# The first layer's direct term moved to its last three stages, product copies ahead of byte codes, and the second layer begun before the last turn

## What is computed

```python
# first layer, K = 4
terms = [x, L @ x]
for _ in range(2, K):
    terms.append(2.0 * (L @ terms[-1]) - terms[-2])
out = einsum('kni,kio->no', stack(terms), weight)
x = layernorm(x + out)
# second layer, as far as it matters here
(adj > 0) @ h, (adj < 0) @ h, adj+ @ h, adj- @ h     # then gates of two GRU cells
```

## The kernel before

| stage | visits | passes | beside the product |
|---|---|---|---|
| start, B | 0-31 | 0; in B also 1 | masks, counts, row sums |
| C | 32-41 | 1, quarter 2 (and two tiles of 3) | codes 0, row sums |
| D | 42-49 | 1, quarter 1 | counts 1, row sums |
| E | 50-57 | 1, and from 52 also 2, quarter 0 | counts 2, codes 1, row sums |
| F | 58-67 | 2, quarters 0 and 1 | codes 2 |
| G | 68-75 | 2, quarter 2 | counts 3, row sums |
| H | 76-83 | 2, quarter 3 | codes 3 |

## Time and profile before

### The profile page before, as it was taken

One profiled execution on the slowest core, in us unless ns is written; L12 is line 12 of the kernel. 1 busy time (PEld: TensorE's weight loads), 2 busy tenths in 40 slices (PEclk: granted clock), 3 DMA queues, 4 the chain that ended last, 5 costly groups with the idle time before them and its releaser, 6 DMA issues. The chain is left out here.

```text
span 1476.3 us, 18448 instructions
## 1 busy us (share of the span) xinstructions
PE 1330.1 (90%) x6874; PEld 592.6 (40%) x6874; DVE 1203.3 (82%) x1560; ACT 984.5 (67%) x919; POOL 222.7 (15%) x150
## 2 busy tenths in 40 slices
PE   5899998999899899999999999989987888888893
PEld 1233334333334354454544554544433433333342
DVE  5898989995865887877977977458688899899997
ACT  0001442894583678567577768677689899999985
POOL 1000000000000000000000001143133445444550
PEclk9999999999999999999999999999979999999995
DMA  9999979988999565544535533143633656556610
GB/s 361 409 409 410 370 264 377 411 346 318 413 410 412 212 234 193 189 147 177 193 134 187 193 138 105 61 148 134 215 114 115 213 158 227 178 166 215 217 54 29
DMA packets 134561, 341.56 MB, mean 231 GB/s; under 512 B 7877, under 2 KB 57481, under 8 KB 134281
## 3 DMA queue, kind: packets, MB, share of 16 engines
q1 hardware_dynamic: 118240, 320.88, 59.4%
q10 hardware_dynamic: 16232, 19.51, 3.9%
HBM read 321.49 MB, written 17.83 MB: 230 GB/s over the span
## 5 line engine op out<-in xcount | busy, mean ns | idle before, releaser
L1088 PE MATMUL ps<-ring,X 128*64 128x512 f32 x512 | 234.1, 605 | 15.4 <-DVE ring L2444 10.2
L1089 PE MATMUL ps<-work,X 128*64 128x512 f32 x512 | 234.2, 605 | 0.0
L844 POOL TENSOR_TENSOR ring<-ring,work 128x1024 f32<-128x1024 f32 x72 | 170.1, 2363 | 223.6 <-DVE work L2836 223.6
L1684 ACT ACTIVATE work<-ring 128x2048 f32<-128x2048 f32 x64 | 122.5, 1913 | 79.4 <-PE ps L1104 31.8
L821 POOL TENSOR_SCALAR work<-ring 128x1024 int16<-128x1024 uint8 x24 | 27.5, 1148 | 963.5 <-DMA ring<-codes 888.2
L951 PE MATMUL ps<-ring,work 128*64 128x512 f32 x704 | 162.6, 610 | 1.5 <-DVE Y L2102 1.5
L2444 DVE TENSOR_SCALAR ring<-ring 128x2048 f32<-128x2048 f32 x64 | 78.4, 1225 | 66.6 <-ACT work L1684 66.1
L1088 PEld LDWEIGHTS ps<-ring,X 128*64 128x64 f32 x512 | 67.1, 139 | 152.1 <-issue 141.8
L2124 DVE TENSOR_TENSOR work<-work,ring 128x1024 f32<-128x1024 f32 (+1 forms) x98 | 108.0, 1102 | 8.5 <-DMA ring<-in_adjT 6.6
L1493 ACT ACTIVATE work<-work,code_bias 128x2048 uint8<-128x2048 bf16 (+1 forms) x32 | 62.2, 1944 | 66.8 <-DVE work L2163 53.5
L1267 PE MATMUL ps<-work 64*128 64x512 f32 x288 | 88.6, 694 | 17.4 <-DVE work L2851 15.9
(11 more groups left out here) (387 smaller groups left out, 2708.1 us busy)
## 6 DMA issues: line engine op xcount, KB each, us to landing
ring<-in_adjT SPq DMA_DIRECT2D x86, 2048.0 KB, 11.3
work<-in_adjT SPq DMA_DIRECT2D x26, 2048.0 KB, 22.3
ring<-in_adjT SPq DMA_DIRECT2D x24, 1024.0 KB, 8.8
ring<-in_adjT SPq DMA_DIRECT2D x48, 512.0 KB, 3.8
ring<-codes SPq DMA_DIRECT2D x32, 512.0 KB, 3.8
ring<-in_adjT SPq DMA_DIRECT2D x64, 256.0 KB, 3.1
codes<-work ACTq DMA_DIRECT2D x32, 256.0 KB, 6.5
codes<-work ACTq DMA_DIRECT2D x64, 128.0 KB, 2.7
```

The source lines that it names most:

```text
L844: nc.gpsimd.tensor_tensor(u.edges[:, cols], u.edges[:, cols], u.angle[:, cols], ALU.mult).then_inc(weighted, 1)
L1088: nc.tensor.matmul(ps[0:F, h, :], rows, ring[:, r, 2 * (m % 2) + i, cols], start=start, stop=stop)
L1089: mm = nc.tensor.matmul(ps[F:P, h, :], rows, negs[:, m % 2, i, cols], start=start, stop=stop)
L1684: nc.scalar.activation(negs[:, pair], ring[:, r, 2 * pair:2 * pair + 2, :], ACT.Relu, scale=-1.0).then_inc(negs_made, 1)
```

## The change

- The direct term moves from visits 37-40 to 60-63 (`FIRST_AT`), with its reads one visit later. Its transfer is now two of 512 KB, one for each half of the partitions, issued by ACT at visit 57, behind the copy of turn 7; x's transposed form lies in T1's room, which has had its last reader then. It uses banks 0 and 1, and turn 11 uses banks 6 and 7.
- The signs of visit 42 wait for nothing of the direct term. `att_weights` goes to banks 2 and 3 and waits for the first counts' read instead of turn 3's. The first normalisation moves one visit later (62).
- On ACT, where the visit ahead of a turn has codes (turns 5 and 9), the copy of the product comes ahead of those codes.
- Turn 11 and its two copies move behind pair 0 of the second layer, on PE behind `mask_products` of pair 0. What pair 0 writes over waits for the room's last reader by name.
- The six rooms are dealt so that the last visits 78, 79, 80, 81, 82 and 83 use rooms 1, 5, 4, 3, 2 and 0. The order in which tiles are loaded is as before.

The diff, cut to its core:

```diff
-        xT_sb = signs_words[0:F, :]
+        xT_sb = work[:, 0:NB * F]
...
-        TURN_BANKS = (0, 4, 0, 4, 0, 6, 4, 0, 6, 4, 0, 4)
+        TURN_BANKS = (0, 4, 0, 4, 0, 6, 4, 0, 6, 4, 0, 6)
...
-        WEIGHTS_AT, ATT_AT, FIRST_AT = C_AT + 2, C_AT + 4, C_AT + 5
-        NORMS_AT = (F_AT + 3, G_AT + 1, H_AT + 1)
+        ATT_AT, FIRST_AT = C_AT + 4, F_AT + 2
+        NORMS_AT = (F_AT + 4, G_AT + 1, H_AT + 1)
...
+        place = {r: p for r, p in zip(sorted(range(RING0), key=lambda r: last_use[r]), (1, 5, 4, 3, 2, 0))}
+        for a in visits:
+            a.slot = place[a.slot]
...
             def first(n):
                 if n == 0:
-                    pe.wait_ge(xT_in, 16)
-                if n < 2:
-                    pe.wait_ge(first_read, 1)
-                else:
+                    pe.wait_ge(xT_in, 32)
+                    pe.wait_ge(turn_read, 8)
+                if n >= 2:
                     pe.wait_ge(first_read, 1 + 2 * (n - 1))
+                rows = slice(n // 2 * F, (n // 2 + 1) * F)
                 for c in range(8):
-                    b = n * 8 + c
-                    mm = nc.tensor.matmul(ps[:, 4 + n % 2, c * F:(c + 1) * F], xT_sb[:, b * P:(b + 1) * P], w_first[:],
+                    b = n % 2 * 8 + c
+                    mm = nc.tensor.matmul(ps[:, n % 2, c * F:(c + 1) * F], xT_sb[rows, b * P:(b + 1) * P], w_first[rows],
...
-            turn(LAST_TURN)
             pe.sem_inc(pair_used, 2)
...
+                    if q == 0 and m == 0:
+                        turn(LAST_TURN)
...
                 if m and a.sign_n == NS:
                     act.wait_ge(based, SLOTS)
-                    act.wait_ge(first_read, 9)
+                    act.wait_ge(first_read, 1)
...
-                if a.t in TURNS_AT:
+                if a.t in TURNS_AT and not visits[a.t - 1].chain:
                     copy_product(act, TURNS_AT.index(a.t))
...
-                if a.t == C_AT:
-                    act.wait_ge(based, SLOTS)
-                    act.wait_ge(counts_made, NS)
-                    act.dma_start(xT_sb, xT).then_inc(xT_in, 16)
...
                 if a.t == F_AT - 1:
                     copy_product(act, 7)
-                if a.t == len(visits) - 1:
-                    copy_product(act, LAST_TURN)
+                    for h in range(2):
+                        act.dma_start(xT_sb[h * F:(h + 1) * F, :], xT[:, h * (N // 2):(h + 1) * (N // 2)]).then_inc(xT_in, 16)
+                if a.chain and a.t + 1 in TURNS_AT:
+                    copy_product(act, TURNS_AT.index(a.t + 1))
                 if a.chain:
                     make_codes(a)
...
-                    act.wait_ge(pair_used, q * PAIRS + m + 1)
+                    if q == 0 and m == 0:
+                        act.wait_ge(tile_multiplied, visits[slot_after[4]].multiplied)
+                    else:
+                        act.wait_ge(pair_used, q * PAIRS + m + 1)
```

More of the change, by code:

```diff
@@ L598, in adjacency_stack @@
             last_use[a.slot] = t
-            a.room = ring[:, a.slot] if a.slot < RING else spare[:, a.slot - RING]
             a.turns = [NQ * p + (a.q if p != 1 else NQ - 1 - a.q) for p in a.passes]
@@ L617, in adjacency_stack @@
                 signed_n += 1
+        place = {r: p for r, p in zip(sorted(range(RING0), key=lambda r: last_use[r]), (1, 5, 4, 3, 2, 0))}
+        for a in visits:
+            a.slot = place[a.slot]
+            a.room = ring[:, a.slot] if a.slot < RING else spare[:, a.slot - RING]
+        slot_after = [max(a.t for a in visits if a.slot == r) for r in range(RING0)]
         turns0 = 3 * NQ
-        slot_after = last_use[0:RING]
         def quarter_blocks(q):
@@ L867, in att_weights @@
                 pe.wait_ge(weights_made, 2)
[L868 to L872 removed]
+                pe.wait_ge(counts_read, 1)
+                nc.tensor.matmul(ps[:, 2, 0:2], gatWT_sb[:], gat_a_sb[:], start=True, stop=True)
+                nc.tensor.matmul(ps[:, 2, F:2 * F + 1], w3_pick[:], w3_words[0:F, :], start=True, stop=True)
+                nc.tensor.matmul(ps[0:F, 2, 3 * F:4 * F + 1], move_pick[:], w3_words[0:F, :], start=True, stop=True)
+                nc.tensor.matmul(ps[:, 3, 0:3 * F], gatWT_sb[:], winT_sb[:], start=True, stop=True).then_inc(
                     gat_ready, 1)
@@ L897, in count @@
                         pe.wait_ge(counts_read, m)
+                        pe.wait_ge(first_read, 1)
                 for h in range(2):
@@ L937, in multiply @@
                     pe.wait_ge(base_read, 2 * NQ)
-                if a.begins[i] and n == 6:
+                if a.begins[i] and n == 10:
                     pe.wait_ge(first_read, 9)
@@ L1687, in _ @@
                         act.wait_ge(negs_made, q * PAIRS + m + 1)
+                        if q == 0 and m == 0:
+                            act.wait_ge(tile_multiplied, visits[slot_after[3]].multiplied)
                         nc.scalar.activation(less[:, pair], negs[:, pair], ACT.Sign).then_inc(less_made, 1)
+                    if q == 0 and m == 0:
+                        copy_product(act, LAST_TURN)
                     make_codes1(q, m)
@@ L2422, in _ @@
                         mine = own_blocks(ring[:, r], s % 2, pair)
+                        if m == 0 and q == 0:
+                            dve.wait_ge(tile_multiplied, visits[slot_after[5]].multiplied)
                         V.tensor_tensor(own, mine, ident[:].unsqueeze(1).broadcast_to([P, 2, P]),
@@ L2438, in _ @@
                     if m % 2:
+                        if q == 0 and m == 1:
+                            dve.wait_ge(tile_multiplied, visits[-1].multiplied)
                         if s // 2 == q:
@@ L2447, in _ @@
                         make_more(q, m, edges).then_inc(masks_made, 1)
+                    if q == 0 and m == 0:
+                        copy_product_dve(LAST_TURN)
                     if q == 0 and m == 2:
```

32 lines of the change are left out of this document (12 added, 20 removed).

## The result

The changed kernel takes 1481.75 us in the median of 20 runs (1475.91 to 1491.39), the kernel before 1477.53 us on the same chip: ratio 1.0029, 95% interval 1.0018 to 1.0041. A second comparison on another chip gave 1483.22 against 1478.16, ratio 1.0037 (1.0023 to 1.0051). It is about 0.3% slower; 1480.3 us was forecast, with a range of 1473.5 to 1485.

A forecast was written before the change was run, and what follows sets the result against it. PE was taken to bound stages D and E and the stretch from pair 0, transfers F to H. Terms -1.65 + 2.9 + 0 + 2.05 = +3.3 us on the median 1477.05 gave 1480.3 us, range 1473.5 to 1485.

The forecast's parts named there:

- Turn 5 and count 42: Stage C to D: count 42 1.65 us earlier, clock loss after PE's idles 2.9 us, so stage E ends 1.25 us later.
- the clock holds: Rival at turn 5: the idles there cost no clock; +0.4 us in all, 1477.5 us; chance 0.15.
- the codes' transfer isn't the gate: Faster rival: visit 42's signs don't wait for that transfer, count starts 4.5 us earlier; down to 1472.3 us; chance 0.17.
- The direct term in stage F: Visits 60 to 63: the added PE and DVE work stays hidden and the stream of tiles unbroken; cost 0.
- the slower rival: Stage F: clock falls behind three narrow pieces, stream of tiles breaks, 3.3 us lost, 1483.7 us; chance 0.23.
- The turn behind pair 0: Start of second layer: turn 11 now stands on PE where it has no gap, nothing gained; +2.05 us.
- Ahead of pair 0: Sign at the passage to the second layer: PE idle for 3 to 5 us before pair 0.

The follow-up runs named there:

- e7: Changed kernel plus useless matmuls on PE around turn 5, 7 ahead and 4 behind; 1479.55 us, ratio 1.0003 to the kernel before.
- after: First profile of the changed kernel, no further edit; the profiled execution spans 1478.4 us (1480.17 as a run).
- e12: Changed kernel run again with no edit, on another chip; 1483.22 us, ratio 1.0037 to the kernel before.
- e1: Changed kernel with turn 11 and its copies back ahead of pair 0; 1482.31 us, ratio 1.0037 to the kernel before.
- e5: Changed kernel with x's transfer cut to an eighth (128 KB in place of 1 MB); 1481.20 us, ratio 1.0025 to the kernel before.
- e9: Changed kernel with the direct term one visit later in stage F; 1483.80 us, ratio 1.0040 to the kernel before.
- e10: Changed kernel, signs of 42 and 68 before codes, turn 11 back, direct term one visit later, useless matmuls around turn 5 (7 and 1); 1470.91 us, ratio 0.9957.
- e6: Changed kernel with signs of visits 42 and 68 ahead of codes of 41 and 67, turn 11 back ahead of pair 0; 1475.27 us, ratio 0.9980.
- e8: Changed kernel, direct term back in stage C, signs of 42 and 68 before codes, turn 11 back ahead of pair 0; 1479.00 us, ratio 1.0009.
- e11: Changed kernel, signs of 42 and 68 before codes, turn 11 back ahead of pair 0, direct term one visit later in F; 1473.19 us, ratio 0.9969.

## Why the prediction was right, and where it wasn't

The total was right (+3.3 forecast, +4.2 in the medians with an interval of 2.7 to 6.1), but that is luck: two terms were set too high and one at nothing, and the errors cancelled. The three below come to +3.4 us; no column tells where the other 0.8 of the medians is. Means are over the table's profiles that have the part in question.

- **Turn 5 and count 42 (forecast +1.25, measured +0.4).** The mechanism stands in each part: DVE's copy at 256.62 (forecast 256.1), idle on both sides of the turn, codes released by a transfer, signs behind them, count at 264.90 (265.2). Counted from the product of visit 31, the count is 2.3 us earlier (1.65 forecast), and the clock costs 2.4 by the first profile and e7 (2.9 forecast): both terms were mis-sized, by 0.7 and 0.5. Over after, e12, e1, e5 and e9, "E" is 155.6 against 155.2. The rival "the clock holds" is wrong, the rival "the codes' transfer isn't the gate" too: it landed after 6.3 us, not under 5.
- **The direct term in stage F (forecast 0, measured +1.9).** This step failed. It took x's megabyte for 2.5 us in a queue that is empty at that time, "through by then". It was issued 4 us ahead of the tile of visit 63, and its halves took 8.2 and 10.1 us, since they shared the engines with tiles; at 412 GB/s its 2.5 us had nowhere to go but into the stream, which from here on is the bound for 115 us. In the kernel before, too, x's transfer (1 MB at 206.0) had taken 8.1 us beside the tiles, a row that the prediction didn't use. "67" is 33.5 us in the three profiles with the term in C, and 34.2 to 36.3 (mean 35.5) in the ten with the term and all of x in F. Besides, the first group of the term stands ahead of visit 61's product, and this alone makes the room for visit 67's tile 1.9 us later (23.7 us behind stage E instead of 21.8); and the slower rival's condition is met in 6 of 8 profiles: the clock falls behind the three narrow pieces, and the room comes free at 377.7 to 381.0 (e12, e1, e5). The rival's price was overstated, since the room and x's transfer delay the same tile, and the later of the two counts: 35.9 us on average with the fall and x, 35.0 with x alone.
- **The turn behind pair 0 (forecast +2.05, measured +1.1).** 94.2 us on average of eight profiles with the late turn, 93.1 in all six without. It falls into two groups: 93.7 to 93.8 where the lower clock ended within 4 us of pair 0's start, 94.5 to 94.8 where it lasted 5 us or more. Without the late turn it is 93.1 in either case (2.7 us of it in e10, over 5 in the others), so the lower clock by itself isn't the difference. Where it ended early, only 0.6 to 0.7 of the turn's 2.05 us come through, where it lasted, 1.4 to 1.7; what hides the rest, PE's wait for masks or another, I haven't traced.
- Ahead of pair 0 PE waited 6.25 us, not 3 to 5: the product of visit 83 ended at 482.9, not up to 485.7. This wait hides it, as forecast.
- Not in the sum at all: the insurance that the late turn gives (e1, e6), and the clock's falls in the later layers, which vary from execution to execution (892.3 to 899.3 us in "rest"), which makes one profile a poor judge of 4 us in 1478.

Left open: a kernel with the term in F and with neither x in the stream nor a fall wasn't run, so that x's 1.6 us and the late room are told apart only by the columns above; nor is it known whether x could travel in stage D or E, where tiles land 7 us and more ahead of use.

## What to carry to other kernels

Work taken off the engine that is busy is worth only what the next gate lets through; here that gate was the order of two instructions on another engine, and swapping them gave 4.2 us to a kernel that the move alone had made as much slower. Each is worth nothing without the other: with the term in C the swap gave nothing over the kernel before (e8), without the swap the move lost, and both together, the turn put back, beat the kernel before (e6 just, e11 clearly). Where a stretch is bound by transfers, bytes that are moved into it are paid, here 1.6 us for x's 2.5, also when its queue looks empty at that moment: ask when the stream begins that isn't to be broken. And an idle of the matrix engine that is made by freeing it has a price of its own in the clock (2.4 us here), which a few useless matmuls can buy back if they are sized to end before the wait does.

## What the runs showed of the hardware that I had not expected

- Three narrow f32 pieces in a row with no idle (eight matmuls each, of 128, 2 and 64 columns, 5.9 us) were followed by the clock's lower level in 6 of 8 profiles; with a wide product ahead of the third, in none of 3.
- The same idle in the same kernel is not always followed by it: in the second layer PE waits for DVE's positive part of a pair (L2453) for 3.53 us up to 624.5 in the changed kernel's first profile and for 3.55 up to 623.9 in e12, and only the former has the lower clock behind it (at 624.8, for 3.4 us).
- Two transfers of 512 KB on ACT's queue, which at the stream's 412 GB/s are 2.5 us together, took 8.2 and 10.1 us beside one stream of 2 MB tiles, and the tile issued behind them took 11.9 to 14.1 us instead of 8.1.
